# An adaLN attention and routed-FFN layer on one core: new setup, the last pair's FFN by sequence, and step orders written out

## The reference

```
h  = layernorm(x) * (1 + scale_a) + shift_a
q, k, v = h Wq', h Wk', h Wv'  (+ biases);  s = |q k'| / 16, causal, softmax
x2 = x + gate_a * (softmax(s) v Wo' + bo)
h2 = layernorm(x2) * (1 + scale_b) + shift_b
cluster scores (8) and tile scores (64) of h2 go through sigmoid and a
8-knot piecewise linear curve; best cluster, then best of its 8 tiles
comp = tanh(gelu(h2 W1 + b1) W2 + b2)                (2 numbers a token)
hh = relu(comp @ w1[tile] + b1[tile]);  mag = hh @ w2[tile] + b2[tile]
y  = layernorm(h2 + mag * directions[tile] * out_scale) * gamma + beta
out = x2 + gate_b * y
```

## Time and profile before

| what | value |
|---|---|
| runs (3), us | 468.45, 471.96, 473.19 |
| median, us | 471.96 |
| the profiled execution, us | 471.67 |
| its span, us | 469.8 |
| mean granted TensorE clock (share of full) | 0.931 |
| busy in the span: PE, DVE, ACT, POOL, us | 399.8, 398.5, 296.5, 67.4 |
| instructions of PE, DVE, ACT, POOL | 2072, 1367, 645, 82 |

### The profile page before, as it was taken

How to read it: one execution, slowest core, us unless ns; L and a number is a source line. 1 busy time by engine, 2 the same in 40 slices (tenths; PEclk the granted TensorE clock), 3 DMA queues, 4 the chain that set the end, 5 groups by cost and what they waited for, 6 DMA issues and landing times.

```text
span 469.8 us, 7656 instructions
## 1 busy us (share of the span) xinstructions
PE 399.8 (85%) x2072; PEld 308.7 (66%) x2072; DVE 398.5 (85%) x1367; ACT 296.5 (63%) x645; POOL 67.4 (14%) x82
## 2 busy tenths in 40 slices
PE   2697899999999999899989998999899999463330
PEld 2555578777777877687768776877677778452220
DVE  4417637387859899999999999999999899999996
ACT  2230365877698769676967697769776976651400
POOL 1002310302020002400250015001400220031040
PEclk9977899999999999999999999999999999796565
DMA  8503102101200213112310231122100210040112
GB/s 292 142 30 105 74 23 79 35 1 45 69 23 1 69 45 114 45 28 86 114 45 25 91 112 47 22 91 86 50 1 1 73 64 1 4 130 0 35 57 89
DMA packets 26234, 28.72 MB, mean 61 GB/s; under 512 B 3888, under 2 KB 21552, under 8 KB 26192
## 3 DMA queue, kind: packets, MB, share of 16 engines
q1 hardware_dynamic: 24160, 26.38, 17.8%
q10 hardware_dynamic: 2032, 1.85, 1.2%
HBM read 19.77 MB, written 8.45 MB: 60 GB/s over the span
## 4 chain that ended last, share of the span: by engine, by line
DVE 45%; PE 42%; issue 8%; ACTq 2%; ACT 2%; DVEq 0%
PE bank L511 8%; PE bank L530 8%; PE bank L490 6%; PE bank L500 6%; PE bank L553 3%; DVE y L1278 3%; DVE y L1246 3%; DVE x L1091 3%; DVE res L1288 3%; DVE st L1254 2%; DVE probs L1077 2%; DVE st L1046 2%; PE bank L520 2%; ACTq L680 2%; DVE v L1070 2%
## 5 line engine op out<-in xcount | busy, mean ns | idle before, releaser
L511 PE MATMUL bank<-h,g 128*128 128x128 f32 (+3 forms) x256 | 80.2, 444 | 4.9 <-DVE v L1070 4.9
L978 POOL TENSOR_TENSOR res<-x,gb_row 128x512 f32<-128x512 f32 x32 | 44.5, 1407 | 268.3 <-DMA out<-res 268.3
L530 PE MATMUL bank<-v,probsT 128*128 128x257 f32 x320 | 79.1, 382 | 0.0
L500 PE MATMUL bank<-m_ga,h 128*128 128x258 f32 x256 | 68.8, 394 | 5.2 <-DVE rows L1360 3.2
L530 PEld LDWEIGHTS bank<-v,probsT 128*128 128x128 f32 x320 | 57.1, 190 | 6.6 <-DVE y L1246 0.3
L490 PE MATMUL bank<-h,a_sb 128*128 128x512 f32 x128 | 60.4, 595 | 0.0
L511 PEld LDWEIGHTS bank<-h,g 128*128 128x128 f32 x256 | 44.7, 195 | 22.1 <-issue 8.5
L500 PEld LDWEIGHTS bank<-m_ga,h 128*128 128x128 f32 x256 | 47.7, 197 | 15.7 <-issue 4.3
L736 ACT ACTIVATE bank<-bank,v 128x128 f32<-128x128 f32 (+1 forms) x64 | 31.7, 495 | 41.4 <-PE bank L511 29.1
L1077 DVE CUSTOM_DVE_ANT_0 probs<-bank,cmask 128x128 f32<-128x128 f32 (+1 forms) x64 | 31.1, 485 | 23.3 <-ACT bank L736 23.3
L742 ACT ACTIVATE probs<-probs,negmax 128x128 f32<-128x128 f32 (+1 forms) x64 | 35.5, 557 | 5.9 <-DVE negmax L1077 5.9
(11 more groups left out here) (167 smaller groups left out, 770.1 us busy)
## 6 DMA issues: line engine op xcount, KB each, us to landing
x<-in_L_attn_x SPq DMA_DIRECT2D x16, 512.0 KB, 3.5
out<-res SPq DMA_DIRECT2D x16, 512.0 KB, 3.0
a_row<-gate_rows SPq DMA_DIRECT2D x16, 256.0 KB, 3.2
gb_row<-gate_rows SPq DMA_DIRECT2D x16, 256.0 KB, 3.2
wide<-in_L_wmod ACTq DMA_DIRECT2D x2, 768.0 KB, 7.6
res<-in_L_attn_Wq SPq DMA_DIRECT2D x1, 256.0 KB, 5.0
res<-in_L_attn_Wk SPq DMA_DIRECT2D x1, 256.0 KB, 7.3
res<-in_L_attn_Wo SPq DMA_DIRECT2D x1, 256.0 KB, 10.1
```

The source lines that it names most:

```text
L500: last = mm(ps[:, 0:VW], h[s][:, c, t * P:(t + 1) * P], m_ga[p % 2][s][:, c, :], start=(c == 0), stop=(c == KC - 1))
L511: last = mm(ps[:, 0:w], g[s][:, c, t * P:(t + 1) * P], h[s][:, c, 0:w], start=(c == 0), stop=(c == KC - 1))
L530: last = mm(ps[:, 0:D + 1], probsT[s][t][:, j * P:(j + 1) * P], v_sb[s][:, j, 0:D + 1], start=(j == 0), stop=(j == t))
L978: gp.tensor_tensor(res[:, 2 * u:2 * u + 2, :], x2[p % 2][s][:, t, :], gb_row[p % 2][s][:, 1:2, :].broadcast_to([P, 2, D]), ALU.add).then_i ...
```

## The change

1. Setup. silu is applied to the transposed c (128x32) instead of 16x256 rows. The modulation weights arrive in three parts: shift and scale of attention, its gate, and the FFN's (now on SP's queue). The gate and gate-times-bias rows of the first two sequences are computed on all 128 partitions by `su_gax`, `sd_gax`, `sd_gab` straight into `a_row`; the others still go through HBM. Copies of the merged matrix, of woT and of the signatures are ScalarE's; signature columns (`sp_sig`) and table constants (`sp_rest`) are POOL's. The four attention biases are loaded from POOL's queue; the table rows from SP's. Two of four `a_xh(0,0,.)` and one `a_h(0,0,.)` are DVE's. Every setup product is a step (`su_`, `sa_`, `sd_`, `sp_`) placed in the engine's order.
2. Groups. The FFN works on groups instead of pairs: pairs 0 to 6 are groups 0 to 6, and the last two sequences are groups 7 and 8, of one sequence (4 tiles) each.
3. Output. A second way is defined (`yh` on ScalarE, `yg` and `yo` on POOL) for groups below BY_DVE; BY_DVE is 0, and no step of it is called. `y_` gets a wait on the previous group's `ob`.
4. Order. The superstep functions, `step` and `run_ahead` are gone; each engine has its calls one after another for the whole run. The bank table is new. In it FFN of group g has HT, FS, HD, CM and the routing up to `oh` beside attention of pair g+1, and OHT, GA, spl, y_, oa, ob at and after the end of that attention, beside pair g+2.

The diff, cut to its core (setup functions, groups, one period of each engine's order and the end of DVE's):

```
+        GROUPS = [(2 * p, 2 * p + 1) for p in range(PAIRS - 1)] + [(B - 2,), (B - 1,)]
+        BY_DVE = 0
...
@@ block.sync
-            load(x_ld[0][1], x_sb[0][1][:, :, :], x_v[1])
             weight(in_o, wo, "Wo")
             weight(in_v, wv, "Wv")
-            for w, name in ((bq, "bq"), (bk, "bk"), (bv, "bv")):
-                load(in_bias, w[:, :], col(ins[f"L0_attn_{name}"]), allow_slow_non_contiguous=True)
-            load(in_bias, bo16[:, :], row(ins["L0_attn_bo"], B))
+            load(x_ld[0][1], x_sb[0][1][:, :, :], x_v[1])
+            load(in_mod2, wmod_sb[:, :, 3 * D:6 * D], wmod_v[:, :, 3 * D:6 * D])
...
@@ block.tensor
+            def su_gax(b):
+                pe.wait_ge(in_mod_ga, 16)
+                pe.wait_ge(cT_rdy, 1)
+                mod_rows(free(f"su_gax{b}", (ga_own[b], 1)), 2, P,
+                         lambda c: c_T[:, c, b:b + 1].broadcast_to([P, P])).then_inc(ga_two[b], 1)
...
+            su_cT(); su_col(); su_A(); su_bias(); su_wo(); su_gax(0); su_ga(); su_sig()
+            XT(0, 0, 0..1); su_M(); su_vb(); G_(0, 0, 0..1); V_(0, 0, 0)
+            XT(0, 1, 0..1); S_(0, 0, 0); su_colf(); PT_(0, 0, 0); su_gax(1); AT(0, 0, 0)
...
+            S_(2, 1, 2..3); PT_(2, 1, 0..1); AT(2, 0, 2..3); AT(2, 1, 0..1); PT_(2, 1, 2..3)
+            AT(2, 1, 2..3); OHT(1, 0..1); GA(1, 0..7); XT(3, 0, 0..1); XT(3, 1, 0..1)
+            BT(1, 0..1); G_(3, 0, 0); V_(3, 0, 0..1); BT(1, 2); G_(3, 0, 1); HT(2, 0)
...
@@ block.scalar
+            b_pt(2, 1, 2..3); a_xh(3, 1, 3); c_oht(1, 0..1); c_ga(1, 0..7); c_gs(2)
+            a_h(3, 0, 0..1); a_h(3, 1, 0..1); c_xh(2, 0..2); b_g(3, 0, 0); c_xh(2, 3..7)
...
@@ block.gpsimd
+            for w, name in ((bq, "bq"), (bk, "bk"), (bv, "bv")):
+                gp.dma_start(w[:, :], col(ins[f"L0_attn_{name}"]), allow_slow_non_contiguous=True).then_inc(in_bias, 16)
+            gp.dma_start(bo_bc[:, :], ins["L0_attn_bo"].rearrange("(o d) -> o d", o=1).broadcast_to([P, D])).then_inc(in_bias, 16)
...
+            def sp_sig():
+                pool.wait_ge(sig_rdy, 1)
+                ts(sig_T, raw_T, 0.3, None, ALU.is_gt)
+                link(ts(sig_tmp, raw_T, -0.3, None, ALU.is_lt))
+                link(tt(sig_T, sig_T, sig_tmp, ALU.subtract))
...
+            def sp_rest():
+                pool.wait_ge(temp_rdy, 1)
...
+                link(ts(table[:, :], t_full[:, :], 1.0, None, ALU.mult))
+                link(tt(t_full[lo, :], t_full[lo, :], table[lo, :].bitcast(F32), ALU.subtract))
+                ts(table[lo, :], t_full[lo, :], 1.0, None, ALU.mult).then_inc(ffn_rdy, 1)
...
+            sp_sig(); ms(0, 0); sp_rest(); ms(0, 1); ms(1, 0..1); ms(2, 0..1); base(0, 0..3)
...
@@ block.vector
+            def sd_gax(b):
+                dve.wait_ge(ga_two[b], 1)
+                gate_rows_of(ga_raw, ga_sign, a_row[0][b][:, 0:D], banks[BANK[f"su_gax{b}"]][:, 0:D]).then_inc(ga_own[b], 1)
+            def sd_rest():
+                dve.wait_ge(in_rest, 16 * 14)
...
+            sd_silu(); sd_st(0); sd_col(); sd_nw(0); a_xh(0, 0, 2..3); sd_st(1); sd_bias(); sd_gax(0)
+            sd_nw(1); a_h(0, 0, 1); a_st(1, 0, 0); sd_m(); a_st(1, 0, 1); sd_vb(); a_st(1, 0, 2)
+            sd_gab(0); sd_ga(); sd_rest(); b_v(0, 0, 0)
...
+            oh(1, 1); b_ri(2, 1, 1..2); b_x2(2, 1, 1..2); b_st(2, 1, 1); b_ri(2, 1, 3); b_st(2, 1, 2)
+            b_x2(2, 1, 3); a_st(4, 0, 0); b_st(2, 1, 3); a_st(4, 0, 1); c_var(2, 0); a_st(4, 0, 2)
+            c_var(2, 1..3); a_st(4, 0, 3); spl(1, 0); c_nw(2, 0); spl(1, 1)
...
+            lob(8, 0..4); oh(8, 0..1); spl(8, 0..5); y_(8, 0..1); y_st(8, 0..1); y_(8, 2..3)
+            y_st(8, 2..3); y_var(8, 0..3); oa(8, 0..1); y_nw(8, 0); oa(8, 2); y_nw(8, 1)
+            oa(8, 3); y_nw(8, 2); ob(8, 0..3)
```

## The result

| kernel | runs, us | median, us | ratio to before (95% interval) |
|---|---|---|---|
| before (beside it) | 468.45, 471.27, 471.96, 473.19 | 471.6 | |
| changed | 484.62, 490.97, 492.51, 492.57 | 491.7 | 1.035 (1.020 to 1.050) |

The changed kernel is slower. The ratio is taken from 484.62 and 490.97 alone, since the two runs at 492.5 count as slow ones, and the profiled execution (492.5 us, span 490.7, granted clock 0.938; before 471.67, 469.8 and 0.931) is one of these two. Forecast were 462 and, at the outside, 473.

A forecast was written before the change was run, and what follows sets the result against it. VectorE was taken to set the period of the steady pairs, TensorE pairs 0 and 1. End of attention at 399.5 plus tail 60.8 gave a span of 460.3, with 1.9 more 462 us; range 456 to 468, at the outside 449 to 473.

The forecast's parts named there:

- step 1: Setup ahead of the first V copy: that copy comes at 31 us instead of 47.4, a gain of 16.4.
- Rival B: Setup: POOL's signature chain or a late bias holds V(0,0,0) to about 40.75, no gain, 471 us; chance 0.17.
- step 5: POOL's new setup at no cost: signature chain takes 7 us, done at 25, its multiply at 27, ahead of V(0,0,0).
- step 2: Pair 0 pays back part of the setup's gain: 36 us instead of 32.8, so pair 1 begins at 67.5.
- step 3: Shorter FFN lag behind attention: pair 1 takes 45 us, pair 2 48, pairs 3 to 6 48.5 each, pair 7 45.
- I take 1.0, nearest to 5.2 less 4: Wait before the spline at each pair's end: gather chain of 5.2 us, covered by some 4 us of other DVE work.
- step 4: After the last attention: DVE busy 52.7 us instead of 60.5, with idle time a tail of 60.8, was 66.7.
- rival D: Tail: the split of the last pair costs more than it wins, +3 to +5 us; no chance of its own.
- The rule of the Trainium skill: VectorE instructions with two SBUF inputs and GpSimd ones reading SBUF exclude each other; sp_rest would add up to 4 us, 466.
- Rival A: Pair ends: gather chain fully covered, POOL's additions harmless; 5 us less in five pairs, 3 elsewhere, 454 us; chance 0.23.
- Rival C: Pair ends: ScalarE late with eight copies, spline uncovered, whole 5.2 us paid in pairs 2 to 7, 487 us; chance 0.10.
- The sign at the root: Whole run: the forecast is wrong at its root if DVE's busy total rises by over 5 us from 398.5.

The follow-up runs named there:

- old_order_split: setup_only up to the end of pair 6's attention, then the changed kernel's order and bank table with the last pair's FFN per sequence; 497.2 us.
- setup_only: Changed kernel up to the end of pair 0's attention, then order and bank table of the kernel before, last pair whole; 458.8 us, ratio 0.973.
- unsplit: The changed kernel with the last pair's FFN whole, its steps behind pair 7's attention in the order of before; 495.3 us.
- act_less: The changed kernel with the gather's ScalarE copies of groups 1 to 5 cut to the spline's parameters; 485.0 us, pairs 3 to 6 at 202.9.
- extra-work runs: Changed kernel with a little VectorE, TensorE or ScalarE work added or repeated in five pairs, one engine and place per run; 486.5 to 494.9 us.

## Why the prediction was wrong

- **Setup (step 1): right.** First V copy 32.6 us, forecast 31 and 29 to 33; in six of the sixteen profiled executions with this head 28.5 to 29.3. Rival B is out.
- **POOL (step 5): right.** The signature chain took 6.9 us (7 taken), though of smaller steps than I had bounded; it ended later than I said, and V(0,0,0) did wait for it, by 0.8 us:

```profile
23.13 0.55 POOL L1782 TENSOR_SCALAR gath<-y 128x128 f32<-128x128 f32 x1 [16.47 <-ACT y L1124]
...
28.98 1.09 POOL L1796 TENSOR_SCALAR f_sb<-gath 128x64 f32<-128x64 f32 x2
29.92 1.26 POOL L1821 TENSOR_TENSOR m_ga<-m_sb,a_row 128x512 f32<-128x512 f32 x1
```

- **Pair 0 (step 2): nearly.** Pair 1 was to begin at 67.5; by the new mark that is 66.2 (before, the mark lies 1.3 ahead of the cut), and it was 69.4, 63 to 64 with the early clock. Off by 3.2.
- **Order (step 3): wrong, and the whole of the sign.** Forecast for pairs 1 to 7 were 45 + 48 + 4 x 48.5 + 45 = 332 us, measured 355.2 (before 322.9, at either cut). The failing sentences are "I take 1.0, nearest to 5.2 less 4" and "The same work and the same stretches by POOL (four base, two ms a pair) give 47.5 + 1.0". I priced the shorter lag as one wait ahead of one instruction, the first spline step. What came instead are 3.4 us a pair of idle time of DVE in many small waits, all over the period; the spline's own wait is 1.5 us of them in pairs 3 to 6, twice. The lead is gone at the two hand-overs that I measured, the one-hot rows and the gather; that the other waits have the same reason is argued. Some 0.8 us a pair are not even idle time: where linked steps stand alone, they overlap their neighbours less. DVE's instructions of pairs 3 to 6 take 235.7 us added up, 239.1 before, but cover 191.7 us against 188.6. That also rules out that POOL stretches DVE's steps more than before, a rival that I had not named. For pair 7 I had PE as the bound, at 45; it took 53.2, with PE busy 49.2 and DVE 47.9.
- **"ScalarE is busy some 36 of 47.5 us, so it can follow": the wrong test.** It still is busy 37 of 51.6, but 9.9 of the 10.3 us at the boundary. An average over the period says nothing of a burst.
- **Tail (step 4): DVE right, idle too small.** DVE 53.3 (forecast 52.7 on a cut that lies 1.3 later), idle 12.8 instead of 8.1. Tail 66.1 on the new cut, against 62.1. The split won in this order, and rival D is out.
- **The rule of the Trainium skill** ("SBUF — State Buffer", "Who interferes with whom") would have given 466 by the constants moved to POOL. That is an estimate, 4 us on top of my sum. The small linked steps at 1.19 us (old_order_split) and the spline step at 1.34 (before) agree with it in kind, but no run here separates sp_rest's share, and at 69.4 or 63.9 us for the same head the sum can't show it.
- **Rival A** is out by the periods. **Rival C was the nearest**, with 487 us, the boundary as its place, ScalarE "late with the eight copies" as its mechanism and periods "over 51" as its sign (51.2 to 52.4 came). It got 0.10, by the same average, and the stated range of 449 to 473 left its 487 out. That its total comes so near is in part luck: one wait of 5.2 us at the spline was not what came.
- **The sign at the root** also spoke: DVE's busy total rose by 17.9 us (398.5 to 416.4). The order has 11.2 of them (396.4 in setup_only, 407.6 in unsplit, 7 instructions more), the split 8.7 (407.6 to 416.4, with 64 instructions; 5.8 were forecast), and the setup gives 2.1 back.

The terms of the miss: head and pair 0 +3.2, pairs 1 to 7 +23.2, tail +4.0, together 30.4 us, which is 490.7 less 460.3. The first of them depends on the execution: at the head's faster pace (63.9 us in setup_only) it would be -2.3.

What stays open is how the 4.2 us a pair divide. Cutting ScalarE's burst by 1.8 us gave 0.9 back (act_less). The rest, I argue from the leads and the linked steps, is mostly the missing distance between producer and consumer, but no run gave it back alone. The bank table is the rival left: the waits of AT(.,0,1) are its own, and it was not tried under the old order, nor the old table under the new.

## What to carry to other kernels

When an order is tightened, price each hand-over between engines by the lead that it had, not the engines by their busy shares: a lead of 2.7 us absorbed 0.9 us of extra ScalarE work for nothing, a lead of 0.1 us passed it on in full. Here the bound engine was already busy 0.99 in the steady pairs, so the shorter lag could win only at the two ends of the run and was paid in every period. Keeping the old steady order and taking the new setup alone gave 458.8 us; the new tail could not be spliced on (old_order_split, 497.2 us). Look at each engine's busy share in slices of a period before saying that it can follow, and at the lead where a slice is full. And check which steps a new bank table makes wait for each other.

## What the runs showed of the hardware

The head of all these kernels is the same list, and it ran at two speeds. PE in the setup of the changed kernel, and in setup_only:

```profile
18.58 3.73 PE L446 MATMUL bank<-wide,c_T 128*128 128x256 f32 x8
...
22.65 1.53 PE L541 MATMUL bank<-ident,xhat 128*128 128x128 f32 x8
24.02 1.89 PE L491 MATMUL bank<-woT,res 128*128 128x256 f32 x8
```

```profile
16.64 2.00 PE L420 MATMUL bank<-wide,c_T 128*128 128x256 f32 x8
...
18.83 1.09 PE L515 MATMUL bank<-ident,xhat 128*128 128x128 f32 x8
19.76 1.89 PE L465 MATMUL bank<-woT,res 128*128 128x256 f32 x8
```

The same eight products of 128x256 take 3.73 and 2.00 us (one starts every 0.43 us in the one, every 0.22 in the other), the transposes 1.53 and 1.09, while the next product is equal, 1.89. The granted clock is given as 1.00 for this stretch in both. The products of Wq and Wk just before them (10.8 to 14.3 us) run at 0.65 us each in both, so PE leaves its slower pace at about 15 us in the one and 24 us in the other. Of sixteen profiled executions ten were late and six early, with the first V copy at 32.1 to 33.4 and at 28.5 to 29.3, and the end of pair 0's attention at 67.2 to 69.7 and at 63.1 to 63.9; 4 to 5 us of any single run are this. What decides between the two isn't shown. That is why the extra-work runs are read by their pairs.

GpSimd's small steps, for which the trace before had no row, took 0.2 to 0.55 us for 128x16 to 128x128, against 1.26 for 128x512.
